# Token buffer of the state-space mixer laid out batch, channel, chunk in place of chunk, channel

## The reference

```python
xn = (x - mu) / jnp.sqrt(var + LN_EPS) * ln_gamma + ln_beta
dA = jnp.exp(-jnp.exp(log_A) * dt[:, None]);  dB = B_param * dt[:, None]
def step(h, u):                       # u: (4, 256), h: (4, 256, 64)
    h = dA * h + dB * u[..., None]
    y = jnp.einsum('dn,bdn->bd', C_param, h) + D_param * u
    return (h, y)
_, ys = jax.lax.scan(step, h0, jnp.swapaxes(xn, 0, 1))      # over 1024 tokens
y = jnp.einsum('btd,ed->bte', jnp.swapaxes(ys, 0, 1), W_out) + b_out
x = x + (layernorm(x) + y)
x = x + cross_attention(ctx, ctx, layernorm(x))
x = x + feed_forward(layernorm(x))    # 256 -> 1024 -> 1024 -> 1024 -> 256
```

## Time and profile before

| | |
|---|---|
| median of 3 runs | 935.07 us (934.67 to 935.14) |
| the profiled execution | 934.08 us |
| its span (first to last instruction) | 932.3 us |
| TensorE busy | 869.6 us, 93% of the span |
| VectorE, ScalarE, GpSimd busy | 55%, 53%, 20% |
| main loop of the mixer | 51.4 to 102.4 us |
| `y_turn` to the first feed-forward matmul | 103.1 to 158.9 us |
| feed-forward net | 158.9 us to the end |

### The profile page before, as it was taken

One profiled execution on the slowest core, in us unless ns is written; L12 is line 12 of the kernel. 1 busy time (PEld: TensorE's weight loads), 2 busy tenths in 40 slices (PEclk: granted clock), 3 DMA queues, 4 the chain that ended last, 5 costly groups with the idle time before them and its releaser, 6 DMA issues.

```text
span 932.3 us, 15096 instructions
## 1 busy us (share of the span) xinstructions
PE 869.6 (93%) x5570; PEld 697.0 (75%) x5570; DVE 514.6 (55%) x927; ACT 493.6 (53%) x761; POOL 183.2 (20%) x201
## 2 busy tenths in 40 slices
PE   1168999899999999999999999999999999999997
PEld 0068867677777778777877887778778777777886
DVE  7987485465446464555555555554555456553411
ACT  2927533476356735764475536653575366635432
POOL 1567800500041002200230014000500050003000
PEclk9679999999999999999999999999999999999999
DMA  9961797500110002000200010001100110001000
GB/s 340 243 162 55 261 387 306 226 1 1 52 45 0 0 22 73 0 0 15 81 0 0 0 73 22 0 0 51 45 0 0 51 45 0 0 23 45 1 1 25
DMA packets 15497, 61.79 MB, mean 66 GB/s; under 512 B 2835, under 2 KB 4502, under 8 KB 14646
## 3 DMA queue, kind: packets, MB, share of 16 engines
q1 hardware_dynamic: 15430, 61.31, 19.0%
q0 software_dynamic: 32, 0.00, 0.0%
HBM read 49.63 MB, written 23.20 MB: 78 GB/s over the span
## 4 chain that ended last, share of the span: by engine, by line
PE 89%; DVE 5%; issue 4%; ACT 1%; POOL 0%; DMA 0%; SPq 0%; DVEq 0%; POOLq 0%
PE pair L1342 51%; PE pair L1329 11%; PE pair L1354 6%; PE pair L1269 4%; PE pair L1280 3%; PE pair L1296 3%; PE pair L470 2%; PE pair L477 2%; PE pair L1289 1%; PE pair L1319 1%; PE pair L1236 1%; PE pair L484 1%; PE pair L539 1%; DVE GG L337 1%; DVE stn L343 1%
## 5 line engine op out<-in xcount | busy, mean ns | idle before, releaser
L950 ACT ACTIVATE vbuf<-pair,scl 128x512 f32<-128x512 f32 x128 | 87.8, 686 | 231.0 <-PE pair L1342 222.1
L1342 PE MATMUL pair<-h2hi,h_turned 128*128 128x512 f32 x512 | 202.6, 396 | 0.0
L1342 PE MATMUL pair<-h2lo,h_turned 128*128 128x512 f32 x512 | 199.6, 390 | 0.0
L1342 PE MATMUL pair<-h1hi,h_turned 128*128 128x512 f32 x384 | 153.1, 399 | 0.0
L1342 PE MATMUL pair<-h1lo,h_turned 128*128 128x512 f32 x384 | 150.0, 391 | 0.0
L1118 DVE TENSOR_TENSOR h1lo<-vbuf,h1hi 128x512 fp32r<-128x512 f32 x80 | 57.7, 722 | 120.1 <-ACT h1hi L951 119.3
L1342 PEld LDWEIGHTS pair<-h2hi,h_turned 128*128 128x128 f32 x512 | 96.2, 188 | 25.2 <-issue 5.9
L1342 PEld LDWEIGHTS pair<-h2lo,h_turned 128*128 128x128 f32 x512 | 96.2, 188 | 19.3
L1118 DVE TENSOR_TENSOR h2lo<-vbuf,h2hi 128x512 fp32r<-128x512 f32 x64 | 44.2, 691 | 107.2 <-ACT h2hi L951 107.1
L1329 PE MATMUL pair<-zThi,w_turned 128*128 128x512 f32 x224 | 92.0, 411 | 2.9 <-DVE vbuf L1142 2.9
L1142 DVE SCALAR_TENSOR_TENSOR vbuf<-pair,scl,sg 128x512 f32<-128x512 f32 x64 | 47.9, 750 | 80.5 <-ACT sg L939 60.8
(11 more groups left out here) (145 smaller groups left out, 1593.3 us busy)
## 6 DMA issues: line engine op xcount, KB each, us to landing
h_turned<-d_h SPq DMA_DIRECT2D x2, 4096.0 KB, 15.1
xres<-in_x SPq DMA_DIRECT2D x8, 512.0 KB, 7.5
tok<-in_xs SPq DMA_DIRECT2D x8, 512.0 KB, 12.2
EE<-alpha_rows SPq DMA_DIRECT2D x16, 256.0 KB, 10.7
ring<-kernel_rows SPq DMA_DIRECT2D x16, 256.0 KB, 4.3
xr<-x_rows SPq DMA_DIRECT2D x8, 512.0 KB, 3.5
out<-xr SPq DMA_DIRECT2D x16, 256.0 KB, 2.1
x_rows<-xres SPq DMA_DIRECT2D x7, 512.0 KB, 12.4
```

The lines of the kernel that those rows point to most:

```text
L950: e.activation(vb[:, s % 2, :], h_ps[s % 4], ACT.Gelu, scale=sc)
L1342: ins = e.matmul(bank, w[:, k, m * P:(m + 1) * P], src[part][:, k, :], start=(k == 0 and part == 0), stop=(k == HC - 1 and part == 1))
```

## The change

`tok` gets the shape partition, batch, channel, chunk: [128, 4, 128, 16]. The 64 values of a channel are now four runs of 16 neighbouring words, the runs 8 KB apart, and the 128 channels of one chunk lie 16 words (64 bytes) apart. The input is arranged so on the host; the 8 transfers stay 512 KB with 4 KB in a piece, two for each batch, and the normalising instructions wait for both. All instructions stay in number, size and order; only the addresses within `tok` (and the wait counts on its loads) change.

```diff
-    tok = nc.alloc_sbuf_tensor_at("tok", [P, BC, P], F32, offset=t["zone_a"])
-    tok5 = tok[:, :, :].rearrange("p (b c) i -> p i b c", b=BATCH)
+    tok = nc.alloc_sbuf_tensor_at("tok", [P, BATCH, P, CH], F32, offset=t["zone_a"])
...
-        for g in range(8):
-            e.dma_start(tok[:, 8 * g:8 * g + 8, :], a["xs"][:, 8 * g:8 * g + 8, :]).then_inc(x_in[g], 16)
+        for b in range(BATCH):
+            for h in range(2):
+                here = slice(L * h, L * h + L)
+                e.dma_start(tok[:, b, here, :], a["xs"][:, b, here, :]).then_inc(x_in[b], 16)
...
-                if c % 8 == 0:
-                    e.wait_ge(x_in[c // 8], 16)
-                e.activation(tok[:, c, :], tok[:, c, :], ACT.Identity, bias=ng[:, c:c + 1], scale=rs[:, c:c + 1]).then_inc(z_rdy, 1)
+                if c % CH == 0:
+                    e.wait_ge(x_in[c // CH], 32)
+                v = tok[:, c // CH, :, c % CH]
+                e.activation(v, v, ACT.Identity, bias=ng[:, c:c + 1], scale=rs[:, c:c + 1]).then_inc(z_rdy, 1)
...
-            e.activation(tok[:, :, OCT * o:OCT * o + OCT], yps[o % 4].rearrange("p (i c) -> p c i", i=OCT), ACT.Copy).then_inc(y_out, 1)
+            e.activation(tok[:, :, OCT * o:OCT * o + OCT, :], yps[o % 4].rearrange("p (i b c) -> p b i c", i=OCT, b=BATCH), ACT.Copy).then_inc(y_out, 1)
...
-                e.tensor_scalar(tok[:, c, :], tok[:, c, :], rs[:, c:c + 1], ng[:, c:c + 1], ALU.mult, ALU.add).then_inc(z_dve, 1)
+                v = tok[:, c // CH, :, c % CH]
+                e.tensor_scalar(v, v, rs[:, c:c + 1], ng[:, c:c + 1], ALU.mult, ALU.add).then_inc(z_dve, 1)
...
-            return tok[:, 2 * SB * b:2 * SB * (b + 1), 32 * q:32 * q + 32]
+            return tok[:, 2 * b:2 * b + 2, 32 * q:32 * q + 32, :]
...
-            e.tensor_tensor(part(b, q), part(b, q), gam[:, 32 * q:32 * q + 32].unsqueeze(1).to_broadcast([P, 2 * SB, 32]), ALU.mult).then_inc(z_h, 1)
+            e.tensor_tensor(part(b, q), part(b, q), gam[:, 32 * q:32 * q + 32].unsqueeze(1).unsqueeze(3).to_broadcast([P, 2, 32, CH]), ALU.mult).then_inc(z_h, 1)
...
-                rhs = tok5[L * h:L * h + L, i, :, 0:CH - 1]
+                rhs = tok[L * h:L * h + L, :, i, 0:CH - 1]
...
-                ins = e.matmul(yps[o % 4][rows, c * BC:(c + 1) * BC], TT[o // 2 % 4][rows, (i % GRP) * L:(i % GRP + 1) * L], tok[rows, :, i], start=(c == 0), stop=False)
+                ins = e.matmul(yps[o % 4][rows, c * BC:(c + 1) * BC].rearrange("p (b c) -> p b c", b=BATCH), TT[o // 2 % 4][rows, (i % GRP) * L:(i % GRP + 1) * L], tok[rows, :, i, :], start=(c == 0), stop=False)
...
-            ins = e.transpose(bank[:, c * P:(c + 1) * P], tok[:, 8 * i + c, :], rev[:, :])
+            ins = e.transpose(bank[:, c * P:(c + 1) * P], tok[:, i // 2, :, 8 * (i % 2) + c], rev[:, :])
...
-    out["xs"] = np.asarray(x).reshape(BC, L, DH, P).transpose(2, 1, 0, 3).reshape(P, BC, P)
+    out["xs"] = np.asarray(x).reshape(BATCH, CH, L, DH, P).transpose(3, 2, 0, 4, 1).reshape(P, BATCH, P, CH)
```

More of the change, by code:

```diff
@@ L367, in norms @@
             for c in range(2 * SB * b + ACT_SHARE, 2 * SB * (b + 1)):
-                if c % 8 == 0 or c == 2 * SB * b + ACT_SHARE:
-                    e.wait_ge(x_in[c // 8], 16)
-                e.tensor_scalar(tok[:, c, :], tok[:, c, :], rs[:, c:c + 1], ng[:, c:c + 1], ALU.mult, ALU.add).then_inc(z_dve, 1)
+                if c % CH == 0 or c == 2 * SB * b + ACT_SHARE:
+                    e.wait_ge(x_in[c // CH], 32)
+                v = tok[:, c // CH, :, c % CH]
+                e.tensor_scalar(v, v, rs[:, c:c + 1], ng[:, c:c + 1], ALU.mult, ALU.add).then_inc(z_dve, 1)
         def part(b, q):
-            return tok[:, 2 * SB * b:2 * SB * (b + 1), 32 * q:32 * q + 32]
+            return tok[:, 2 * b:2 * b + 2, 32 * q:32 * q + 32, :]
         def gamma(n):
@@ L383, in beta @@
             e.wait_ge(z_h, n + 1)
-            e.tensor_tensor(part(b, q), part(b, q), bet[:, 32 * q:32 * q + 32].unsqueeze(1).to_broadcast([P, 2 * SB, 32]), ALU.add).then_inc(z_b, 1)
+            e.tensor_tensor(part(b, q), part(b, q), bet[:, 32 * q:32 * q + 32].unsqueeze(1).unsqueeze(3).to_broadcast([P, 2, 32, CH]), ALU.add).then_inc(z_b, 1)
         for k in range(4):
```

## The result

The change makes the kernel slower by 0.44%: 939.24 us median (20 runs) against 935.11 us (20 runs) for the kernel before, a ratio of 1.0044 with a 95% interval of 1.003 to 1.0058, about 4.1 us. The forecast of 940.2 us lies 1 us above it. The cause it named is not the one that the trace shows: the transposes cost next to nothing, and two other places together, the normalising and a late load of TensorE's code, cost 4.3 us, where the transposes were to cost 5.7.

What follows compares the result with a forecast made beforehand. TensorE was taken to bound the kernel (busy 93% of the span). From 934.08 us profiled, -0.6 (loop) + 0 (normalising) + 5.7 (transposes) gave 939.2, and 940.2 us for the median, which lies 1.0 us higher; range 934.6 to 944.0.

Steps and rivals of the forecast that it cites:

- Part 3: Transposes after the main loop: `tok` weights 64 bytes apart cost 0.115 us more a transpose, +5.7 us in sum.
- the upper bound: Transposes: 128 scattered weight words at 1.75 ns give 0.224 us each; the other bound, weight load hidden, was 0.109.
- the weight load hides: Rival on the transposes: scattered weights cost nothing, 934.5 us, up to 938 with the normalising's range; chance 0.18.
- The ratio of four: Main loop's streamed `tok`: a word 512 bytes from the last costs about 1.75 ns, long streams near 0.4 ns a column.
- calls 0 to 7: Eight transpose calls, 0.92 us each before hiding: 0 and 1 +1.5, 2 and 3 +1.8, 4 +0.6, 5 0, 6 and 7 +1.8.
- Part 2: Normalising before the loop: first matmul 0 to 4 us later, but 0 taken for the end, range 0 to +4.
- the upper end: Normalising: words 64 bytes apart add 0.13 us to each of VectorE's 24 instructions, 1.6 us for each dozen.
- the stand: TensorE's 2.79 us stop for code after the loop's start; forecast to shrink below 1 us, absorbing the later start.
- the head start isn't forgiven: Rival on the normalising: all of its delay stands, +3.7 us, giving 943.9 us; chance 0.12.
- Part 1: Main loop: shorter `state` and `within` passes gain little, as code loading, ScalarE and VectorE limit octets; -0.6 us, range -2 to +1.
- What an earlier or later ring transfer does to a code load behind it: Main loop: an effect on code loading that the prediction could not fix better than -1 to +1 us.
- ScalarE's 2.35 us: Main loop: ScalarE's busy time an octet, taken as one of three limits on what shorter passes could gain.

Runs made afterwards that it cites:

- The experiment that does this part alone: Kernel before, with only the transposes' weights taken from words 64 bytes apart: 934.64 us, 1.0007 (0.9993 to 1.0021).
- the flat normalising: Changed kernel with the normalising instructions put back on 128 neighbouring words (output not the reference's): 937.1 us, 1.0029 (1.0014 to 1.0044).
- held copies: Changed kernel with the feed-forward weights' copies waiting for the last octet's output, not its last `state` matmul: 936.23 us, 1.0022 (1.0013 to 1.0032).
- the loop part alone: Changed kernel with normalising on neighbouring words and feed-forward weights' copies waiting for the last octet's outputs: 933.36 us, 0.9998 (0.9986 to 1.001).

## Why the prediction was right, and where it was not

The range held the time and the direction was right. The sum was right by compensation. Its terms, one by one:

- **Part 3, +5.7 us: wrong, and the step that failed was the choice of the upper bound** ("weights and streamed columns are read out of the same memory"). Transposes stand 0.113 us apart, where 0.224 was taken and 0.109 was the lower bound. The experiment that does this part alone gives 1.0007. The condition of the rival "the weight load hides", at 0.18, was the true one; its time, 934.5 us, did not come, since the normalising and the late load had their price. The rule of the Trainium skill on lines of 16 bytes (Advanced Engine Details and Errata, Memory Cachelines), which I let speak against the change here, shows in the streamed operand of this case and not in its weights. The ratio of four that was set beside it compared different matmuls; the same `state` step fell from 0.103 to about 0.058 us with runs of 16 words, a ratio of 1.8. The later terms (calls 0 to 7 and what hides them) fell with it.
- **Part 2, 0 taken: wrong at the forgiving.** ScalarE's twenty take 10.0 us for 7.8, +0.11 us each; no run shows the upper end that the prediction took for ScalarE, nor the figure under it. VectorE's dozen takes 3.48 us, +0.04 us each, where the upper end, 0.13, gave 4.5. The first matmul came 1.5 us later in the pair of traces and 2.7 us later on average, inside 0 to 4. But the stand did not take it up: of the 2.7 us, 2.3 are left behind it. I had argued that a TensorE that comes later meets free DMA engines. In eleven traces whose first matmul lies anywhere between 49.45 and 53.1 us the first code load starts 5.4 to 6.1 us behind it, so the wait for the load moves along with TensorE; only the two latest starts, 53.75 and 54.79, have it after 4.9 and 4.7 us. In the changed kernel the DMA share was still 1.03 up to 57.7 us and 0.51 in the stand. The normalising alone measures +2.7 us (1.3 to 4.0). The rival "the head start isn't forgiven" had the mechanism, with 3.7 for what measured 2.7. The half clock behind the stand, which I had gone, is there: 0.50 in 61.7 to 64 us.
- **Part 1, -0.6 us: the reading of the loop was right, its consequence was cut short.** Passes shortened about as said (at full clock `state` records to 217 and `within` to 236 ns, for 225), stops of 0.6 to 1.9 us appeared at nearly every piece, and the octets kept their pace on average (single ones took from 1.87 to 3.5 us, so ScalarE's 2.35 us is no floor for one octet); without the other two causes the loop is worth nothing (0.9998). What the step left out was its last load. "What an earlier or later ring transfer does to a code load behind it" was in the range, with 1 us; the transfer that mattered was another one, the copies of the feed-forward weights that SP issues at the end of the loop, and it costs 2 us or so (1.0044 down to 1.0022; 1.0029 down to 0.9998 with the flat normalising, 2.9 us). And with longer stops the clock fell at times, which I had not priced: 0.88 in 85.2 to 98.9 us.

Added up by what the runs measured: the normalising costs 2.7 us in the kernel before, 2.2 in the changed kernel with held copies (1.0022 against 0.9998) and 1.4 without (1.0044 against 1.0029); the late load 2.1 to 2.9; the passes 0, the transposes 0.3 or less. Each of these has about 1.3 us of uncertainty or more. Both causes together are 4.3 us by the ratios, against 4.1 measured. That the forecast lies within 1 us of this is luck: 5.7 us at the wrong place stood for 4.3 us at two others, of which one was priced at 0 and the other had no term.

Why short passes don't pay, by the records of the code loads and with a piece counted as 256 matmul and weight-load records: with held copies, from 85 to 101 us, a load starts 1.1 to 1.3 us after TensorE has gone on with a piece (up to 1.9 in the trace of the loop part alone), and the next piece's first matmul follows 2.2 to 2.5 us behind the start of the load. So 256 instructions take 3.4 to 4.1 us however short the passes are. In the kernel before the loads started 1.1 to 1.3 us into a piece and the next piece followed 2.3 us behind each, in pieces of 3.4 to 3.6 us, and the passes alone need 3.4 us for the 10.7 channels of a piece. It stood at both limits at once, which is why its trace shows no stop there. The Trainium skill (Runtime: NRT & Kernel Launch, section Instruction fetch mechanics) says that code comes in blocks of 16 KiB, 256 instructions, and that crossing one is mostly hidden. The trace agrees on the size; hidden it is behind the mixer, where from 131 to 256 us the loads come 21 to 30 us apart and no stop at the start of a piece is over 0.3 us, and not here, where 256 instructions last 2.7 to 3.4 us. That the floor lies in the load itself, not in the issuing of instructions, is what the positions of the stops say, and the step of 2.2 to 2.9 us from a load's start to the next piece, which stays whether passes are short or long; what sets the start of a load within its piece is not known.

## What to carry to other kernels

- When an engine's stream shows "issue" stops at even distances in instructions, count the instructions in a piece and compare its running time with the time from one code load to the next: below that, shorter instructions buy nothing, and fewer instructions would be the thing to try (not tried here). Look at the records of the loads too: a piece that just fits shows no stop and has no room either.
- A layout is paid by everyone who touches the buffer. Price each user by rows that move the same kind of operand: the streamed columns of a matmul say nothing about the loading of weights.
- When an edit shifts TensorE by a microsecond or two, look at which bulk transfers start nearby, and whether a code load changes sides with one of them.

## What the runs showed of the hardware that I had not expected

- Weights of 4-byte words 64 bytes apart load as fast as the stream needs: 0.113 us for a 128 x 128 transpose, with neighbours 0.109. Scattered words did cost the streamed operand: `state` steps took about 0.103 us with 512 bytes between words, and 0.055 to 0.06 in runs of 16 words (no run streams words 64 bytes apart).
- Words 64 bytes apart, read and written in place, cost ScalarE 0.50 us for 128 elements instead of 0.39, and VectorE 0.29 instead of 0.25.
- A code load that falls behind bulk copies came about 5 us late (107.8 us, where 102.5 was due), for 16 KB that are on the way for about 1.1 us.
- A wait on a semaphore that has long been reached has a record of 51 ns on TensorE. It cost about 40 ns of running time where a channel's passes took 0.23 us, and next to nothing where they took 0.32; in both kernels it made the code loads come later in their pieces (9 and 11.5 us in all, for two waits a channel).
- Code that TensorE runs again is not loaded again: in the trace of before, the feed-forward net goes through a loop of about 1000 TensorE instructions, 97 us a turn, and from 256.2 to 863.8 us there is no code load.
